# One block of weights and biases for each expert, and three buffers for the dense items: a graph network and a mixture of experts in one launch

## The chip, the cores and the metric

The kernel runs on one core of a Trainium2 chip. The metric is the device time of one execution in microseconds (us); lower is better. Each comparison is against runs of the kernel before on the same chip.

## The reference

Sixteen graphs of 512 nodes with 128 features go through two residual layers, x = x + gnn(layernorm(x)) and x = x + ffn(layernorm(x)), in float32. The second layer is the one that the change is about:

```
xn = (x - mu) * rsqrt(var + EPS) * gamma + beta
top_vals, top_idx = top_k(xn @ Wr + br, 2)          # 2 of 8 experts for each of 8192 tokens
w_full = one_hot-weighted softmax(top_vals)
for e in range(8):
    h = gelu(xn @ W1[e] + b1[e])                    # 128 -> 256
    y_e = h @ W2[e] + b2[e]                         # 256 -> 128
    y = y + y_e * w_full[..., e, None]
```

The first layer is, for each graph, two convolutions over the nodes (17 taps in the second), a message step over a 512x512 matrix exp(-dist) * adj, and a GRU cell with gates from both.

## The kernel before, in words

One program is written by hand for the five engines, with explicit semaphores. TensorE (PE) does the products and transposes, ScalarE (ACT) the gelus and the copies out of PSUM, VectorE (DVE) the splits of float32 values into two parts, the layer norms and the router, GpSimd (POOL) the indirect DMAs, SyncE (SP) issues every other DMA, each engine in the order in which its program is written. An engine's program is in order: what stands behind a wait waits too.

**Graph loop.** `iteration(g)` runs 16 times. Besides graph g's network it finishes graph g-1 (`tail`), routes its tokens, and writes their normalized rows to the lists of their experts in HBM (`routed`). From graph 4 on (`FIRST`) it also works on four **tiles** (`SLOTS`) of 256 routed rows, each with one expert's weights. A tile needs three loads, which SP issues a graph ahead in `tile_loads`: its rows (`xt`, 144 KB), `w1_t` (256 KB: W1 in a high and a low part) and `w2_t` (136 KB: W2, b1, b2 and a one-hot row). Which expert and which rows are read from a small table with two `value_load`s. There are `RING` = 8 buffers of each. On PE a tile is `turn` (transposes of `xt`), `hidden` (six products with W1, lines 573 to 575; waits for `w1_in`), `second` (W2, line 598; behind the gelu) and `back` (transposes, line 606). DVE weighs the result and POOL adds it to the output rows.

**Last stage.** Behind the graph loop stand 50 items, numbered 48 to 97: the last 18 tiles (tiles 48 to 65), and 32 **dense items**, in which each expert's weights are put to all 512 tokens of the last two graphs (q = 0 and 1) in halves of 256, with no routing. The order is worked out in `last_items`. PE runs at step i: `turn` of item i+2 (tiles only), `hidden` or `dense_hidden` of item i+1, `second` of item i, `back` of item i-1. A dense item's weights come in ten loads (`DENSE_LOADS`), each for the two or four items of one expert. They go into two buffers (`wd1`, `wd2`, by k % 2):

```
load k                       0   1   2   3   4   5   6   7   8   9
first item that reads it    53  56  59  66  73  79  86  90  94  96
last item that reads it     54  58  64  71  78  84  89  93  95  97
```

`dense_loads(k)` waits until the last item of load k-2 is through (`pe_y`, `yT_done`), then issues two DMAs. Loads 0 and 1 are issued behind the graph loop, before the stores of padding rows; the others stand in one order with the tiles' loads (`loads_in_order`, sorted by the item that each waits for): tiles 48 to 60, **load 2**, tile 61, tile 62, load 3, tiles 63 and 64, load 4, tile 65, loads 5 to 9. Tiles 48 to 55 wait for POOL's adds (`added`), later ones for items. `dense_hidden` waits for `wd1_in`, `xd_split` and the gelu of an earlier item; ACT's gelu of a dense item waits for `wd2_in`.

**The blocks in HBM** are written once: at graph 0 and 1, ACT and DVE fill `w1_s` and `w2_s` in SBUF (W1 scaled by gamma and split, W2, the biases), and SP stores them with two DMAs (lines 461 and 462) into `w1_all` and `w2_all`; the first tile's loads wait for that (`w12_stored`).

At step AT_NORM = 6 and AT_ROUTE = 9 of the last stage (items 54 and 57) the last graph's rows are normalized and its router's logits are computed (line 777); DVE's `choose` and `place`, at steps 10 and 11, turn them into weights.

Of the kernel before, what the change touches and what calls it, by code (L numbers as in the profile page):

```python
# [15 lines left out]
P = 128  # L16
# [80 lines left out]
W1COLS = 4 * P  # L97
X_B1 = 2 * P
X_B2 = X_B1 + HALVES
X_OH = X_B2 + 1  # L100
XCOLS = 272
# [43 lines left out]
def gnn_moe(nc, x, adj_t, weights, vectors, consts, pads, routed, w1_all, w2_all, out):  # L145
# [4 lines left out]
    with ExitStack() as ctx:  # L150
# [22 lines left out]
        w1_t = [sb(f"w1_t{i}", [P, W1COLS], F32R) for i in range(RING)]  # L173
        w2_t = [sb(f"w2_t{i}", [P, XCOLS]) for i in range(RING)]
# [7 lines left out]
        wd1 = [sb(f"wd1_{i}", [P, W1COLS], F32R) for i in range(2)]  # L182
        wd2 = [sb(f"wd2_{i}", [P, XCOLS]) for i in range(2)]
# [147 lines left out]
        wd1_in = [sem(f"wd1_in{i}") for i in range(2)]  # L331
        wd2_in = [sem(f"wd2_in{i}") for i in range(2)]
        xt_in = [sem(f"xt_in{i}") for i in range(RING)]
        w1_in = [sem(f"w1_in{i}") for i in range(RING)]
        w2_in = [sem(f"w2_in{i}") for i in range(RING)]
# [74 lines left out]
        def _(sp):  # L410
# [14 lines left out]
            sp.dma_start(w2_s[:, :, 0:2 * P],  # L425
# [16 lines left out]
            def dense_loads(k):  # L442
                if k >= 2:
                    sp.wait_ge(pe_y, last_of_load(k - 2) + 1)
                    sp.wait_ge(yT_done, last_of_load(k - 2) + 1)
                e = DENSE_LOADS[k][0]
                sp.dma_start(wd1[k % 2][:].bitcast(F32), w1_all[e, :, :]).then_inc(wd1_in[k % 2], 16)
                sp.dma_start(wd2[k % 2][:], w2_all[e, :, :]).then_inc(wd2_in[k % 2], 16)

            def iteration(g, tail, more, moe):  # L450
                d = g - 1

                def next_loads(j):
                    n, slot, loads = tile_of(g + 1, j)
                    if n >= RING:
                        sp.wait_ge(added, 16 * TT * (n - RING + 1))
                    tile_loads(slot, *chosen[j])

                if g == 1:
                    sp.wait_ge(w12_ready, 2)  # L460
                    sp.dma_start(w1_all.rearrange("e p h -> p e h"), w1_s[:].bitcast(F32)).then_inc(w12_stored, 16)
                    sp.dma_start(w2_all.rearrange("e p h -> p e h"), w2_s[:]).then_inc(w12_stored, 16)
                if tail:
                    sp.wait_ge(x1_ready, d + 1)
                    if d < ROUTED:
                        sp.dma_start(out_v[d], x1[:]).then_inc(out_set, 16)
                if more:
                    sp.wait_ge(a_prod, NT * g + NT)
                    sp.dma_start(adj[:], adj_v[g + 1]).then_inc(adj_loaded, 16)
                if g < GRAPHS - 2:  # L470
                    sp.wait_ge(xl_ready, g + 2)
                    sp.dma_start(x_ln[:], x_v[g + 2]).then_inc(x_ln_loaded, 16)
                if FIRST - 1 <= g < GRAPHS - 1:

                    sp.wait_ge(tab_step, TAB_STEPS * (g - 2))
                sp.dma_start(x_res[:], x_v[g]).then_inc(x_res_loaded, 16)
                if g == FIRST - 1:
# [15 lines left out]
            for k in range(2):  # L493
                dense_loads(k)
# [31 lines left out]
        def _(pe):  # L526
# [97 lines left out]
            def iteration(g, tail, more, moe):  # L624
# [10 lines left out]
                def tile_b(j):  # L635
                    if moe:
                        second(tile_of(g, j)[0], w2_t[tile_of(g, j)[1]])
# [115 lines left out]
            for i in range(-2, len(items) + 1):  # L753
# [9 lines left out]
                if 0 <= i < len(items):  # L763
                    item = items[i]
                    second(item[0], w2_t[item[2]] if is_tile(item) else wd2[item[4] % 2])
# [16 lines left out]
        def _(act):  # L782
# [15 lines left out]
            def gelu(m, w2):  # L798
# [3 lines left out]
                for h in range(HALVES):  # L802
                    last = nc.scalar.activation(ge[m % 2][:, h, :], HID[bank_set(m)][:, h * TILE:(h + 1) * TILE], ACT.Gelu,  # L803
                                                bias=w2[:, X_B1 + h:X_B1 + h + 1])
                last.then_inc(gelu_done, 1)

            def results(m, w2):
# [3 lines left out]
                nc.scalar.activation(yT[m % 2][:], YO[bank_set(m)][:, 0:TILE], ACT.Identity,  # L811
                                     bias=w2[:, X_B2:X_B2 + 1]).then_inc(yT_done, 1)
# [27 lines left out]
            def iteration(g, tail, more, moe):  # L840
# [6 lines left out]
                def tile_gelu(j):  # L847
                    if moe:
                        n, slot, loads = tile_of(g, j)
                        act.wait_ge(w2_in[slot], loads)  # L850
                        gelu(n, w2_t[slot])

                def tile_results(j):
                    n = tile_of(g, 0)[0] + j
                    if moe and n >= 0:
                        results(n, w2_t[n % RING])
# [31 lines left out]
                if is_graph(g, 0):  # L888
                    act.wait_ge(w1_loaded, 16)
                    nc.scalar.activation(w1_s[:, :, 0:2 * P], w1_raw[:].rearrange("p (e h) -> p e h", e=EXPERTS),  # L890
# [47 lines left out]
            results(STREAMED - 1, w2_t[(STREAMED - 1) % RING])  # L938
            for i in range(-2, len(items)):
# [117 lines left out]
        def _(dve):  # L1057
# [300 lines left out]
            def iteration(g, tail, more, moe):  # L1358
# [5 lines left out]
                if is_graph(g, 1):  # L1364
                    dve.wait_ge(w1_hi, 1)
                    nc.vector.scalar_tensor_tensor(
                        out=w1_s[:, :, 2 * P:4 * P], in0=w1_raw[:].rearrange("p (e h) -> p e h", e=EXPERTS),
                        scalar=vec[:, V_GAMMA:V_GAMMA + 1], in1=w1_s[:, :, 0:2 * P].bitcast(F32), op0=ALU.mult,
# [3 lines left out]
                    nc.vector.tensor_tensor(w2_s[:, :, X_B1:X_B1 + HALVES],  # L1372
# [3 lines left out]
                    nc.vector.tensor_copy(w2_s[:, :, X_B2], vec[:, V_EB2:V_EB2 + EXPERTS])  # L1376
                    nc.vector.tensor_copy(w2_s[:, :, X_OH:X_OH + EXPERTS],
                                          cst[:, C_OH:C_OH + 64].rearrange("p (e f) -> p e f", f=EXPERTS))
                    nc.vector.memset(w2_s[:, :, X_OH + EXPERTS:], 0.0).then_inc(w12_ready, 1)
# [243 lines left out]
```

## Time and profile before

| | |
|---|---|
| device time, 3 runs | median 666.71 us (663.08 to 667.06) |
| the profiled execution | 669.05 us, of which the span of the trace is 667.3 us |
| granted TensorE clock, mean over the span | 0.987 |
| busy: PE, its weight loads, DVE, ACT, POOL | 93%, 79%, 75%, 63%, 52% of the span |
| HBM read, written | 75.85 MB, 30.51 MB |
| DMA issued by SP | 83.28 MB in 82736 packets |

The profiled execution is 2.3 us above the median of the runs. Times inside the trace are counted from the start of the span. A granted clock of 1.00 is 2.4 GHz, 0.5 is 1.2 GHz. "Idle before" is the time that an engine stood still before an instruction, and behind the arrow is what the trace takes for its releaser; "issue" is said where the trace shows none. SP's DMA issues are listed with the time that SP took to issue them, not with their landing.

### The profile page before, as it was taken

What the parts mean: (1) busy time and instruction counts of PE and PEld (TensorE: products, weight loads), DVE (VectorE), ACT (ScalarE), POOL (GpSimd) and SP (SyncE); (2) the same over time, 40 slices, a digit from 0 to 9 for tenths busy, and PEclk for the clock granted to TensorE, in tenths of its full rate; (3) what the DMA queues carried; (4) which work ended last, traced back from release to release, by engine and by line L of the source; (5) the groups of instructions that cost most, each with busy time, mean ns of one, the idle gap of its engine ahead of it and who ended that gap; (6) DMA issues with size and microseconds to landing.
All of it is one profiled execution on the core that took longest, in us unless ns stands there. A gap on an engine that the chain in (4) does not pass through costs nothing.

```text
span 667.3 us, 13068 instructions
## 1 busy us (share of the span) xinstructions
PE 623.3 (93%) x3784; PEld 530.2 (79%) x3784; DVE 498.2 (75%) x2050; ACT 418.4 (63%) x824; POOL 344.6 (52%) x273
## 2 busy tenths in 40 slices
PE   3799898989999999999999999999999988799996
PEld 2679687777979797979797888888888777688874
DVE  6958888888888888888888888888888755333322
ACT  4544546485858485858485858585767546466663
POOL 3200314145847474748474747574757545556750
PEclk9898999999999999999999999999999979899999
DMA  8327231538379747474755666666555578863341
GB/s 305 115 92 245 82 124 52 179 101 232 75 203 340 195 117 189 122 191 120 182 130 152 154 153 159 156 156 158 149 140 153 147 184 200 224 144 53 52 77 57
DMA packets 105399, 101.04 MB, mean 151 GB/s; under 512 B 8896, under 2 KB 83904, under 8 KB 105024
## 3 DMA queue, kind: packets, MB, share of 16 engines
q1 hardware_dynamic: 82736, 83.28, 40.4%
q0 software_dynamic: 22592, 16.92, 16.7%
q8 instruction: 31, 0.51, 0.3%
q14 instruction: 40, 0.33, 0.1%
HBM read 75.85 MB, written 30.51 MB: 159 GB/s over the span
## 4 chain that ended last, share of the span: by engine, by line
PE 63%; DVE 17%; issue 7%; DMA 5%; POOL 4%; ACT 3%; SPq 0%; another core or an unknown queue 0%; DVEq 0%; ACTq 0%; POOLq 0%
PE Y L598 9%; PE G L708 5%; PE C L530 5%; PE C L531 5%; PE C L532 5%; PE G L530 4%; PE G L532 4%; PE G L531 4%; PE G L598 4%; POOL routed L1013 2%; DMA x_ln<-x 2%; DMA out<-y_t,xt 2%; PE H L573 2%; PE Y L606 2%; PE H L574 2%
## 5 line engine op out<-in xcount | busy, mean ns | idle before, releaser
L978 POOL DMA_INDIRECT out<-y_t,xt x96 | 157.5, 1641 | 130.7 <-DMA out<-y_t,xt 85.9
L1013 POOL DMA_INDIRECT routed<-row,at_u x112 | 118.6, 1059 | 119.8 <-DVE at_u L1207 86.9
L530 PE MATMUL C<-cv_h,w_hi 128*128 128x256 f32 (+1 forms) x432 | 131.2, 304 | 2.2 <-DVE cv_l L1068 1.3
L531 PE MATMUL C<-cv_l,w_hi 128*128 128x256 f32 (+1 forms) x432 | 124.5, 288 | 0.0
L532 PE MATMUL C<-cv_h,w_lo 128*128 128x256 f32 (+1 forms) x432 | 124.3, 288 | 0.0
L530 PEld LDWEIGHTS C<-cv_h,w_hi 128*128 128x128 f32 x432 | 82.7, 191 | 4.8 <-issue 2.2
L531 PEld LDWEIGHTS C<-cv_l,w_hi 128*128 128x128 f32 x432 | 82.7, 191 | 1.3
L532 PEld LDWEIGHTS C<-cv_h,w_lo 128*128 128x128 f32 x432 | 82.7, 191 | 0.7
L598 PE MATMUL Y<-ge,w_t 128*128 128x256 f32 x228 | 62.0, 395 | 6.0 <-DVE y_t L1307 3.5
L708 PE MATMUL G<-ex,msg_t 128*128 128x512 f32 x128 | 58.9, 603 | 0.3 <-ACT gh L901 0.3
L598 PEld LDWEIGHTS Y<-ge,w_t 128*128 128x128 f32 x228 | 39.4, 192 | 24.0 <-issue 20.5
L803 ACT ACTIVATE ge<-H,w_t 128x256 f32<-128x256 f32 x114 | 47.8, 473 | 5.9 <-PE H L575 5.4
L708 PEld LDWEIGHTS G<-ex,msg_t 128*128 128x128 f32 x128 | 23.1, 190 | 23.5 <-issue 23.0
L910 ACT CAST cv_h<-G 128x512 fp32r<-128x512 f32 x16 | 9.4, 586 | 51.4 <-PE G L708 51.4
L530 PE MATMUL G<-xlT_h,w_hi 128*128 128x512 f32 x96 | 39.9, 415 | 1.5 <-DVE xlT_l L1138 1.5
L1413 DVE TENSOR_TENSOR ex<-ex,adj 128x512 f32<-128x512 f32 x64 | 39.7, 677 | 0.0
L532 PE MATMUL G<-xlT_h,w_lo 128*128 128x512 f32 x96 | 38.3, 399 | 0.0
L531 PE MATMUL G<-xlT_l,w_hi 128*128 128x512 f32 x96 | 38.2, 398 | 0.0
L573 PE MATMUL H<-xT_h,w_t 128*128 128x256 f32 x114 | 36.3, 319 | 0.6 <-DVE xT_l L1286 0.6
L811 ACT ACTIVATE yT<-Y,w_t 128x256 f32<-128x256 f32 x57 | 26.9, 472 | 12.1 <-PE Y L598 8.5
L575 PE MATMUL H<-xT_h,w_t 128*128 128x256 f32 x114 | 32.5, 285 | 0.0
L574 PE MATMUL H<-xT_l,w_t 128*128 128x256 f32 x114 | 32.4, 284 | 0.0
(264 smaller groups left out, 1692.8 us busy)
## 6 DMA issues: line engine op xcount, KB each, us to landing
w_t<-w_all SPq DMA_DIRECT2D x66, 256.0 KB
adj<-adj_t SPq DMA_DIRECT2D x16, 1024.0 KB
xt<-routed SPq DMA_DIRECT2D x66, 144.0 KB
w_t<-w_all SPq DMA_DIRECT2D x66, 136.0 KB
x_ln<-x SPq DMA_DIRECT2D x16, 256.0 KB, 6.3
x_res<-x SPq DMA_DIRECT2D x16, 256.0 KB
out<-x SPq DMA_DIRECT2D x15, 256.0 KB
wd<-w_all SPq DMA_DIRECT2D x10, 256.0 KB
```

Source lines behind the costliest of these rows:

```text
L530: pe.matmul(psum, hi(w), rhs_h, start=start, stop=False)
L531: pe.matmul(psum, hi(w), rhs_l, start=False, stop=False)
L532: return pe.matmul(psum, lo(w), rhs_h, start=False, stop=stop)
L573: pe.matmul(half, w[:, h * P:(h + 1) * P], x_h, start=True, stop=False)
L574: pe.matmul(half, w[:, h * P:(h + 1) * P], x_l, start=False, stop=False)
L575: last = pe.matmul(half, w[:, (2 + h) * P:(3 + h) * P], x_h, start=False, stop=True)
L598: last = pe.matmul(YO[bank_set(m)][:, 0:TILE], w2[:, h * P:(h + 1) * P], ge[m % 2][:, h, :], start=(h == 0), stop=(h == HALVES - 1))
L708: last = pe.matmul(G0[:], msg_t[:, j, :], ex[:, j, :], start=(j == 0), stop=(j == NT - 1))
L803: last = nc.scalar.activation(ge[m % 2][:, h, :], HID[bank_set(m)][:, h * TILE:(h + 1) * TILE], ACT.Gelu, bias=w2[:, X_B1 + h:X_B1 + h + 1])
L978: nc.gpsimd.indirect_dma_start(out=out, out_offset=bass.IndirectOffsetOnAxis(ap=xt[j][:, t, R_ID:R_ID + 1].bitcast(U32), axis=0), in_=y_t[ ...
L1013: nc.gpsimd.indirect_dma_start(out=routed, out_offset=bass.IndirectOffsetOnAxis(ap=at_u[:, n:n + 1], axis=0), in_=row[:, n // TOP, :], in_ ...
L1413: nc.vector.tensor_tensor(ex[:, j, :], ex[:, j, :], adj[:, j, :], ALU.mult).then_inc(a_prod, 1)
```

## The change

The four column ranges of an expert's block are put side by side in one row of 784 floats (3136 bytes): W1 high and low, W2, b1, b2 and the one-hot row. `w1_s` and `w2_s` become `w_s`, `w1_all` and `w2_all` become `w_all`, `w1_t` and `w2_t` become `w_t`. The size is what both had together (2048 + 1088 bytes a row). One DMA stores the blocks, and one loads a tile's or a dense item's block; there is one semaphore for it, and PE, ACT and DVE all wait for that. The dense items' blocks have three buffers instead of two: load k waits for the last item of load k-3, loads 0 to 2 are issued behind the graph loop, and in the order of the rest load 3 stands where load 2 stood, 4 where 3 stood, and so on. All products, activations and vector operations keep their shapes and order.

```diff
@@ -94,11 +94,13 @@
-W1COLS = 4 * P
-X_B1 = 2 * P
+X_W2 = 4 * P
+X_B1 = X_W2 + 2 * P
 X_B2 = X_B1 + HALVES
 X_OH = X_B2 + 1
-XCOLS = 272
+XCOLS = X_B1 + 16
...
+DENSE_BUFFERS = 3
@@ -164,14 +166,12 @@
             w1_raw = once("w1_raw", [P, 16 * P])
-            w1_s = once("w1_s", [P, EXPERTS, W1COLS], F32R)
-            w2_s = once("w2_s", [P, EXPERTS, XCOLS])
+            w_s = once("w_s", [P, EXPERTS, XCOLS], F32R)
             beta_b = once("beta_b", [P, P])
...
         xt = [sb(f"xt{i}", [P, TT, ROW]) for i in range(RING)]
-        w1_t = [sb(f"w1_t{i}", [P, W1COLS], F32R) for i in range(RING)]
-        w2_t = [sb(f"w2_t{i}", [P, XCOLS]) for i in range(RING)]
+        w_t = [sb(f"w_t{i}", [P, XCOLS], F32R) for i in range(RING)]
         yT = [sb(f"yT{i}", [P, TILE]) for i in range(2)]
@@ -179,8 +179,7 @@
         own_w = [sb(f"own_w{i}", [P, TT]) for i in range(4)]
-        wd1 = [sb(f"wd1_{i}", [P, W1COLS], F32R) for i in range(2)]
-        wd2 = [sb(f"wd2_{i}", [P, XCOLS]) for i in range(2)]
+        wd = [sb(f"wd{i}", [P, XCOLS], F32R) for i in range(DENSE_BUFFERS)]
         xd_h = [sb(f"xd_h{i}", [P, NODES], F32R) for i in range(DENSE)]
@@ -396,7 +393,7 @@
-            at = [(last_of_load(k - 2), 1, k) for k in range(2, len(DENSE_LOADS))]
+            at = [(last_of_load(k - DENSE_BUFFERS), 1, k) for k in range(DENSE_BUFFERS, len(DENSE_LOADS))]
             at += [(number.get(n - RING, STREAMED), 0, n) for n in range(STREAMED, STREAMED + LAST)]
@@ -430,9 +427,8 @@
                     xt_in[j], 16)
-                sp.dma_start(w1_t[j][:].bitcast(F32), w1_all[bass.ds(e, 1), :, :].rearrange("e p h -> p (e h)")).then_inc(
-                    w1_in[j], 16)
-                sp.dma_start(w2_t[j][:], w2_all[bass.ds(e, 1), :, :].rearrange("e p h -> p (e h)")).then_inc(w2_in[j], 16)
+                sp.dma_start(w_t[j][:].bitcast(F32), w_all[bass.ds(e, 1), :, :].rearrange("e p h -> p (e h)")).then_inc(
+                    w_in[j], 16)
@@ -440,12 +436,12 @@
             def dense_loads(k):
-                if k >= 2:
-                    sp.wait_ge(pe_y, last_of_load(k - 2) + 1)
-                    sp.wait_ge(yT_done, last_of_load(k - 2) + 1)
+                if k >= DENSE_BUFFERS:
+                    sp.wait_ge(pe_y, last_of_load(k - DENSE_BUFFERS) + 1)
+                    sp.wait_ge(yT_done, last_of_load(k - DENSE_BUFFERS) + 1)
                 e = DENSE_LOADS[k][0]
-                sp.dma_start(wd1[k % 2][:].bitcast(F32), w1_all[e, :, :]).then_inc(wd1_in[k % 2], 16)
-                sp.dma_start(wd2[k % 2][:], w2_all[e, :, :]).then_inc(wd2_in[k % 2], 16)
+                sp.dma_start(wd[k % DENSE_BUFFERS][:].bitcast(F32), w_all[e, :, :]).then_inc(
+                    wd_in[k % DENSE_BUFFERS], 16)
@@ -458,8 +454,7 @@
                     sp.wait_ge(w12_ready, 2)
-                    sp.dma_start(w1_all.rearrange("e p h -> p e h"), w1_s[:].bitcast(F32)).then_inc(w12_stored, 16)
-                    sp.dma_start(w2_all.rearrange("e p h -> p e h"), w2_s[:]).then_inc(w12_stored, 16)
+                    sp.dma_start(w_all.rearrange("e p h -> p e h"), w_s[:].bitcast(F32)).then_inc(w12_stored, 16)
                 if tail:
@@ -475,7 +470,7 @@
                 if g == FIRST - 1:
-                    sp.wait_ge(w12_stored, 32)
+                    sp.wait_ge(w12_stored, 16)
                     sp.wait_ge(pads_stored, 16)
@@ -490,7 +485,7 @@
-            for k in range(2):
+            for k in range(DENSE_BUFFERS):
                 dense_loads(k)
@@ -578,25 +573,25 @@
                 pe.wait_ge(xT_split, n + 1)
-                pe.wait_ge(w1_in[j], loads)
+                pe.wait_ge(w_in[j], loads)
                 if m > 0:
                     pe.wait_ge(gelu_done, m if m <= STREAMED else m - 1)
-                hidden_products(HID[bank_set(m)], w1_t[j], xT_h[n % 2][:], xT_l[n % 2][:])
+                hidden_products(HID[bank_set(m)], w_t[j], xT_h[n % 2][:], xT_l[n % 2][:])
...
                 pe.wait_ge(xd_split, q + 1)
-                pe.wait_ge(wd1_in[k % 2], 16 * (k // 2 + 1))
+                pe.wait_ge(wd_in[k % DENSE_BUFFERS], 16 * (k // DENSE_BUFFERS + 1))
                 pe.wait_ge(gelu_done, m - 1)
                 cols = slice(u * TILE, (u + 1) * TILE)
-                hidden_products(HID[bank_set(m)], wd1[k % 2], xd_h[q][:, cols], xd_l[q][:, cols])
...
-            def second(m, w2):
+                hidden_products(HID[bank_set(m)], wd[k % DENSE_BUFFERS], xd_h[q][:, cols], xd_l[q][:, cols])
...
+            def second(m, w):
                 pe.wait_ge(gelu_done, m + 1)
...
                 for h in range(HALVES):
-                    last = pe.matmul(YO[bank_set(m)][:, 0:TILE], w2[:, h * P:(h + 1) * P], ge[m % 2][:, h, :],
-                                     start=(h == 0), stop=(h == HALVES - 1))
+                    last = pe.matmul(YO[bank_set(m)][:, 0:TILE], w[:, X_W2 + h * P:X_W2 + (h + 1) * P].bitcast(F32),
+                                     ge[m % 2][:, h, :], start=(h == 0), stop=(h == HALVES - 1))
                 last.then_inc(pe_y, 1)
@@ -943,14 +938,14 @@
                     if is_tile(item):
-                        act.wait_ge(w2_in[item[2]], item[3])
-                        gelu(item[0], w2_t[item[2]])
+                        act.wait_ge(w_in[item[2]], item[3])
+                        gelu(item[0], w_t[item[2]])
                     else:
-                        act.wait_ge(wd2_in[item[4] % 2], 16 * (item[4] // 2 + 1))
-                        gelu(item[0], wd2[item[4] % 2])
+                        act.wait_ge(wd_in[item[4] % DENSE_BUFFERS], 16 * (item[4] // DENSE_BUFFERS + 1))
+                        gelu(item[0], wd[item[4] % DENSE_BUFFERS])
                 if i >= 0:
                     item = items[i]
-                    results(item[0], w2_t[item[2]] if is_tile(item) else wd2[item[4] % 2])
+                    results(item[0], w_t[item[2]] if is_tile(item) else wd[item[4] % DENSE_BUFFERS])
                 if i == AT_SUM + 2:
@@ -1287,10 +1282,10 @@
             def own_weight(n, j, loads):
-                dve.wait_ge(w2_in[j], loads)
+                dve.wait_ge(w_in[j], loads)
                 dve.wait_ge(xt_in[j], loads)
                 nc.vector.tensor_tensor(pick_w[n % 4][:], xt[j][:, :, R_W:R_W + EXPERTS],
-                                        over(w2_t[j][:, X_OH:X_OH + EXPERTS], 1, [P, TT, EXPERTS]),
+                                        over(w_t[j][:, X_OH:X_OH + EXPERTS].bitcast(F32), 1, [P, TT, EXPERTS]),
                                         ALU.mult).then_inc(own_step, 1)
...
```

## Rows read from the trace of the kernel before

**Rows 1.** Busy time by stretch: from:to, length, PE, PEld, DVE, ACT, POOL, clock, DMA share, GB/s.
```profile
461.30:494.90 33.60, 33.45 (x211) 28.70 (x211) 28.81 (x125) 23.26 (x47) 21.45 (x16) 1.00 0.59 148
538.80:549.00 10.20, 7.86 (x33) 6.51 (x33) 5.23 (x19) 4.33 (x11) 4.67 (x3) 0.67 0.79 208
...
571.50:580.40 8.90, 4.47 (x20) 3.73 (x19) 1.27 (x6) 1.68 (x4) 6.54 (x6) 0.81 0.96 239
580.40:654.30 73.90, 71.64 (x442) 61.85 (x441) 28.28 (x119) 49.23 (x117) 43.23 (x39) 1.00 0.46 82
654.30:667.30 13.00, 7.15 (x38) 5.49 (x38) 3.14 (x10) 4.33 (x10) 0.00 (x0) 1.00 0.25 72
```

**Rows 2.** Waits of PE in the last stage: total us, times, longest.
```profile
PE G L573 <- issue: 4.4, 1, 4.4
...
PE H L573 <- issue: 0.9, 1, 0.9
```

**Rows 3.** SP's issues in order of time: start us, us to issue.
```profile
517.13 0.46 SPq L448 DMA_DIRECT2D wd<-w_all  x1
...
536.09 0.41 SPq L431 DMA_DIRECT2D xt<-routed  x1
...
538.88 0.38 SPq L431 DMA_DIRECT2D xt<-routed  x1
539.46 0.33 SPq L433 DMA_DIRECT2D w_t<-w_all  x1
539.97 0.33 SPq L435 DMA_DIRECT2D w_t<-w_all  x1
...
572.28 0.38 SPq L447 DMA_DIRECT2D wd<-w_all  x1
...
653.82 0.33 SPq L447 DMA_DIRECT2D wd<-w_all  x1
```

**Rows 4.** PE in order of time, last stage: start us, us, [idle before].
```profile
545.18 0.56 PE L573 MATMUL G<-xT_h,w_t 128*128 128x256 f32 x1
...
571.33 0.42 PE L541 MATMUL H<-cst,xt 128*128 128x128 f32 x2
576.18 0.50 PE L573 MATMUL G<-xd_h,wd 128*128 128x256 f32 x1 [4.43 <-issue]
...
582.82 1.10 PE L598 MATMUL Y<-ge,w_t 128*128 128x256 f32 x4
...
652.13 1.10 PE L598 MATMUL G<-ge,wd 128*128 128x256 f32 x4 [0.16 <-DVE x_d L1320]
...
654.32 1.10 PE L598 MATMUL Y<-ge,wd 128*128 128x256 f32 x4 [0.15 <-DVE x L1320]
...
656.49 0.36 PE L573 MATMUL H<-xd_h,wd 128*128 128x256 f32 x1 [0.86 <-issue]
...
657.28 1.03 PE L598 MATMUL G<-ge,wd 128*128 128x256 f32 x4
...
659.51 1.10 PE L598 MATMUL Y<-ge,wd 128*128 128x256 f32 x4 [0.27 <-DVE x L1320]
```

**Rows 5.** DVE in order of time behind the long wait.
```profile
579.87 0.42 DVE L1307 TENSOR_TENSOR adj<-G,own_w 128x256 f32<-128x256 f32 x1 [6.90 <-PE G L606]
...
582.06 0.61 DVE L1320 SCALAR_TENSOR_TENSOR x_d<-Y,w_d,x_d 128x128 f32<-128x128 f32 x2
```

**Rows 6.** The last instruction of POOL in order of time.
```profile
643.37 1.56 POOL L999 DMA_INDIRECT out<-x_ln,ids  x1 [0.30 <-issue]
```

**Rows 7.** SP and PE in order of time: a graph's first tile, issue and use.
```profile
328.37 0.35 SPq L433 DMA_DIRECT2D w_t<-w_all  x1
...
338.89 0.47 PE L573 MATMUL H<-xT_h,w_t 128*128 128x256 f32 x1
```

**Rows 8.** The `x_ln` tile: issue to landing of its loads, 256 KB each.
```profile
DMA to landing us min/median/max: 2.8/6.3/7.5
```

**Rows 9.** DMA issues by line: the second of the two stores, us to landing.
```profile
w_all<-w_s SPq DMA_DIRECT2D x1, 1088.0 KB, 11.6
```

More of the change, by code:

```diff
@@ L142, in pad_rows, with gnn_moe @@
     return r
-def gnn_moe(nc, x, adj_t, weights, vectors, consts, pads, routed, w1_all, w2_all, out):
+def gnn_moe(nc, x, adj_t, weights, vectors, consts, pads, routed, w_all, out):
     x_v = x.rearrange("g (t p) d -> g p t d", p=P)
@@ L330, in gnn_moe @@
         tab_step, xd_hi, xd_split = map(sem, ("tab_step", "xd_hi", "xd_split"))
-        wd1_in = [sem(f"wd1_in{i}") for i in range(2)]
-        wd2_in = [sem(f"wd2_in{i}") for i in range(2)]
+        wd_in = [sem(f"wd_in{i}") for i in range(DENSE_BUFFERS)]
         xt_in = [sem(f"xt_in{i}") for i in range(RING)]
-        w1_in = [sem(f"w1_in{i}") for i in range(RING)]
-        w2_in = [sem(f"w2_in{i}") for i in range(RING)]
+        w_in = [sem(f"w_in{i}") for i in range(RING)]
         pe_xtT, xT_hi, xT_split, pe_h, gelu_done, pe_y, yT_done, pe_yT, own_step, own_done, y_done, added = map(
@@ L424, in _ @@
             sp.dma_start(w1_raw[:], weights[:, W1 * P:(W1 + 16) * P]).then_inc(w1_loaded, 16)
-            sp.dma_start(w2_s[:, :, 0:2 * P],
+            sp.dma_start(w_s[:, :, X_W2:X_W2 + 2 * P].bitcast(F32),
                          weights[:, W2 * P:(W2 + 16) * P].rearrange("p (e h) -> p e h", e=EXPERTS)).then_inc(w2_loaded, 16)
@@ L636, in tile_b @@
                     if moe:
-                        second(tile_of(g, j)[0], w2_t[tile_of(g, j)[1]])
+                        second(tile_of(g, j)[0], w_t[tile_of(g, j)[1]])
                 if is_graph(g, 1):
@@ L764, in _ @@
                     item = items[i]
-                    second(item[0], w2_t[item[2]] if is_tile(item) else wd2[item[4] % 2])
+                    second(item[0], w_t[item[2]] if is_tile(item) else wd[item[4] % DENSE_BUFFERS])
                 if 0 <= i - 1:
@@ L796, in turned, with gelu @@
                 nc.scalar.copy(xT_h[n % 2][:], XT[s][:, 0:TILE]).then_inc(xT_hi, 1)
-            def gelu(m, w2):
+            def gelu(m, w):
                 act.wait_ge(pe_h, m + 1)
@@ L803, in gelu, with results @@
                     last = nc.scalar.activation(ge[m % 2][:, h, :], HID[bank_set(m)][:, h * TILE:(h + 1) * TILE], ACT.Gelu,
-                                                bias=w2[:, X_B1 + h:X_B1 + h + 1])
+                                                bias=w[:, X_B1 + h:X_B1 + h + 1].bitcast(F32))
                 last.then_inc(gelu_done, 1)
-            def results(m, w2):
+            def results(m, w):
                 act.wait_ge(pe_y, m + 1)
@@ L811, in results @@
                 nc.scalar.activation(yT[m % 2][:], YO[bank_set(m)][:, 0:TILE], ACT.Identity,
-                                     bias=w2[:, X_B2:X_B2 + 1]).then_inc(yT_done, 1)
+                                     bias=w[:, X_B2:X_B2 + 1].bitcast(F32)).then_inc(yT_done, 1)
             def normalized_rows(d):
@@ L849, in tile_gelu @@
                         n, slot, loads = tile_of(g, j)
-                        act.wait_ge(w2_in[slot], loads)
-                        gelu(n, w2_t[slot])
+                        act.wait_ge(w_in[slot], loads)
+                        gelu(n, w_t[slot])
                 def tile_results(j):
@@ L855, in tile_results @@
                     if moe and n >= 0:
-                        results(n, w2_t[n % RING])
+                        results(n, w_t[n % RING])
                 act.wait_ge(pe_s, g + 1)
@@ L889, in iteration @@
                     act.wait_ge(w1_loaded, 16)
-                    nc.scalar.activation(w1_s[:, :, 0:2 * P], w1_raw[:].rearrange("p (e h) -> p e h", e=EXPERTS),
+                    nc.scalar.activation(w_s[:, :, 0:2 * P], w1_raw[:].rearrange("p (e h) -> p e h", e=EXPERTS),
                                          ACT.Copy, scale=vec[:, V_GAMMA:V_GAMMA + 1]).then_inc(w1_hi, 1)
@@ L937, in _ @@
             d = GRAPHS - 1
-            results(STREAMED - 1, w2_t[(STREAMED - 1) % RING])
+            results(STREAMED - 1, w_t[(STREAMED - 1) % RING])
             for i in range(-2, len(items)):
@@ L1366, in iteration @@
                     nc.vector.scalar_tensor_tensor(
-                        out=w1_s[:, :, 2 * P:4 * P], in0=w1_raw[:].rearrange("p (e h) -> p e h", e=EXPERTS),
-                        scalar=vec[:, V_GAMMA:V_GAMMA + 1], in1=w1_s[:, :, 0:2 * P].bitcast(F32), op0=ALU.mult,
+                        out=w_s[:, :, 2 * P:4 * P], in0=w1_raw[:].rearrange("p (e h) -> p e h", e=EXPERTS),
+                        scalar=vec[:, V_GAMMA:V_GAMMA + 1], in1=w_s[:, :, 0:2 * P].bitcast(F32), op0=ALU.mult,
                         op1=ALU.subtract).then_inc(w12_ready, 1)
@@ L1371, in iteration @@
                     dve.wait_ge(pe_b1, 1)
-                    nc.vector.tensor_tensor(w2_s[:, :, X_B1:X_B1 + HALVES],
+                    nc.vector.tensor_tensor(w_s[:, :, X_B1:X_B1 + HALVES].bitcast(F32),
                                             H0[:, 0:16].rearrange("p (e h) -> p e h", h=HALVES),
@@ L1375, in iteration @@
                                             ALU.add).then_inc(b1_set, 1)
-                    nc.vector.tensor_copy(w2_s[:, :, X_B2], vec[:, V_EB2:V_EB2 + EXPERTS])
-                    nc.vector.tensor_copy(w2_s[:, :, X_OH:X_OH + EXPERTS],
+                    nc.vector.tensor_copy(w_s[:, :, X_B2].bitcast(F32), vec[:, V_EB2:V_EB2 + EXPERTS])
+                    nc.vector.tensor_copy(w_s[:, :, X_OH:X_OH + EXPERTS].bitcast(F32),
                                           cst[:, C_OH:C_OH + 64].rearrange("p (e f) -> p e f", f=EXPERTS))
-                    nc.vector.memset(w2_s[:, :, X_OH + EXPERTS:], 0.0).then_inc(w12_ready, 1)
+                    nc.vector.memset(w_s[:, :, X_OH + EXPERTS:].bitcast(F32), 0.0).then_inc(w12_ready, 1)
                 def tile_split(j):
@@ L1616 @@
     routed = nc.dram_tensor("routed", (DUMMY + LAST * TILE, ROW), F32, kind="Internal").ap()
-    w1_all = nc.dram_tensor("w1_all", (EXPERTS, P, W1COLS), F32, kind="Internal").ap()
-    w2_all = nc.dram_tensor("w2_all", (EXPERTS, P, XCOLS), F32, kind="Internal").ap()
+    w_all = nc.dram_tensor("w_all", (EXPERTS, P, XCOLS), F32, kind="Internal").ap()
     out = nc.dram_tensor("out", (TOKENS + LAST * TILE, P), F32, kind="ExternalOutput").ap()
-    gnn_moe(nc, *args, routed, w1_all, w2_all, out)
+    gnn_moe(nc, *args, routed, w_all, out)
     result = run_bass_kernel_spmd(nc, [arrays], core_ids=[0])
```

## The prediction

> **What bounds the kernel now.** I read the busy time by stretch first, because the share over the whole span hides the stages [rows 1]. In the graph loop a graph takes 33.6 us and PE is busy in 33.45 of them at the full clock: only less PE work could shorten it, and the change takes none away. The last stage is different. PE is busy in 4.47 of 8.9 us between 571.5 and 580.4, in 7.86 of 10.2 between 538.8 and 549, and in 7.15 of the last 13. In the two low stretches the granted clock was 0.81 and 0.67, so TensorE went partly at 1.2 GHz. Next come the waits of PE in that stage [rows 2]: the longest is one of 4.4 us ahead of line 573, and line 573 also has one of 0.9 us. Both have "issue" as releaser, which says only that the trace names none. PE's rows in order of time [rows 4] show both in front of a `dense_hidden` (it reads `xd_h` and `wd`), at 576.18 and at 656.49, and SP's rows [rows 3] show a `wd` load issued shortly before each: at 572.28 (load 2) and at 653.82 (load 9). The other things that `dense_hidden` waits for, the split rows and an earlier gelu, were there long before. So I take both for waits on loads, issue to first product 3.9 and 2.67 us. Why they are issued late is in the code. Load 2 stands in SP's queue behind thirteen tiles' loads, and SP needs 2.79 us for a tile (536.09 to 538.88 [rows 3]). Load 9 has to wait for item 93 to leave its buffer and is read by item 96.
>
> **The third buffer, load 2.** Load 2 goes out beside loads 0 and 1, whose last issue is at 517.13 [rows 3], some 59 us before it is read. The long wait goes. The transposes ahead of it start at 571.33 and take some 0.15 us of PE's time when it doesn't stop, so `dense_hidden` of item 59 can start at about 571.5. What follows would run as in the undisturbed part. From the start of six products to the `second` behind them is 0.79 us (656.49 to 657.28). An item costs 2.10 us (582.82 is `second` of item 60, 654.32 that of item 94: 71.5 us over 34 items) [rows 4]. `second` of item 60 is then due at 571.5 + 0.79 + 2 x 2.10 = 576.5. It was at 582.82, so **6.3 us** are won. Of these 4.7 are the wait itself. The other 1.6 are the work behind it that went at 1.2 GHz: the first product behind the wait takes 0.50 us, the same one at 656.49 takes 0.36 [rows 4]. From 580.4 to 654.3, with PE at work, the clock was 1.00 [rows 1]; without the standstill I see nothing to lower it.
>
> What is late next there? DVE's router work for the last graph. DVE begins to weigh item 57 at 579.87 and its weighing of item 58 starts at 582.06, ends at 582.67, and `second` of item 60 starts right behind, at 582.82 [rows 5, 4]. This is a chain of 2.95 us from `back` of item 57, and it moves forward with that. `back` of item 57 would end at about 571.5 + 0.8 (six products) + 1.0 (`second`) + 0.4 (two transposes, 0.42 at 571.33) = 573.7, so DVE allows item 60 at 576.7. That takes 0.2 away: **6.1 us**.
>
> **The third buffer, load 9.** It now waits for item 89, seven items before it is read, or 15 us, against the 2.67 that it needs. The last items stand 2.19 us apart (652.13 and 654.32, `second` of items 93 and 94). At that pace item 96 would come at 654.32 + 4.38 = 658.70; it came at 659.51 [rows 4], so **0.8 us** are won. Loads 3 to 8 had five to nine items of lead and get ten to fifteen; PE shows no third wait of this kind [rows 2], so they bring nothing.
>
> **One load for two.** SP saves one issue for each tile, 539.97 - 539.46 = 0.51 us [rows 3], so over thirteen tiles its queue gets 6.6 us shorter until POOL's adds hold it up. With load 2 out of the queue no item waits for SP. Cover: PE's own work. In the graph loop SP saves 2 us a graph beside a full PE: nothing. Against that, `hidden` now waits for the whole block, where it waited for W1 alone. The block is issued where W1 was, and it can't land later than W2's load did, if the bytes move at the same pace; so `hidden` waits for at most 0.5 us more than now. The tightest tile is 49: issue of W1 at 539.46, products at 545.18, 5.7 us [rows 3, 4] against 3.9 for the slowest dense load. In the loop a first tile has 10.5 us (328.37 to 338.89 [rows 7]). Bounds: nothing, and a gain of up to 1 us if the stretch from 538.8 to 549 is held by these loads in part. I take nothing.
>
> **The stores, the writes in `w_s`, the added issue.** One store for two of the same bytes; the second of the two took 11.6 us to land [rows 9] around 65 us, and its first reader is issued at 127. Between nothing and 0.3 us in the graphs where SP issues it; I take nothing. The vector writes go to rows with another pitch, with the same elements: nothing. The third dense load adds about 0.5 us to SP at 518, in a pause before the padding stores. PE's weights and ACT's biases come from the same kind of buffer.
>
> **The end.** POOL's last add starts at 643.37 [rows 6] and would be over at 645; the new end of PE's work is near 657, so POOL isn't next. The final store behind the last item stays.
>
> **Sum.** 6.1 + 0.8 = 6.9 us. The profiled execution took 669.05, so it would take 662.15; the median of the runs is 2.3 lower, and I subtract the same from it: 666.71 - 6.9 = **659.8 us**, 1.03% less.
>
> **A rule beside it.** The Trainium skill, "DMA: Bandwidth & Descriptors", section "Anatomy of one DMA", gives a DMA some 2.0 us plus its bytes at 436 GB/s; by that load 2 (256 KB) would have been ready 2.6 us after its issue, at 574.9. The trace agrees for load 9 (2.67) and not for load 2 (3.9, in a stretch with a DMA share of 0.96 [rows 1]). An estimate from that page makes the wait 3.4 us, and the sum 5.6 us and not 6.9.
>
> **Rivals.**
> (B) *The wait is shorter in a usual execution.* Load 2 met busy DMA engines. If it lands as load 9 did, in 2.67 us, PE waits 1.2 us less; the clock may then also stay up for part of the work behind it. The gain is 4.2 to 5.7 us: 661 to 662.5. For it: the runs are faster than the profiled execution by 2.3 us, and something in them must be shorter. Against it: the same queue order and the same traffic exist in each of them. The Trainium skill, "TensorE: Matmul & The Clock Gate", section "Part 1: The HAM clock gate", says that the point at which the clock changes varies from run to run with the same kernel; no run here shows that yet. By that the 1.5 us for the clock could be anything between nothing and all of it.
> (C) *Another wait takes the place.* DVE's `choose` and ACT's gap step now come while PE is at full pace; if their chain of 2.95 us grows by one item, or the clock falls all the same, 2 to 3 us are given back: about 662.5.
> (D) *The releaser isn't the load.* The trace names none. Then only load 9's 0.8 us are left: 665.9. Against it stand two pairs of issue and start.
> (E) *Shorter queue, more gain.* If the stretch from 538.8 to 549 is held by tile loads, up to 1 us, and the clock's share behind it, up to 2: 657.
> (F) *Slower.* The joint block lands late where only W1 was waited for. Place: the first tile of eleven graphs (all with tiles but the first) and tiles 49 to 52. Price: every microsecond by which a block needs more than 10.5 us costs 11 us in the loop [rows 7]; above 5.7 us each of tiles 49 to 52 waits too, and the clock falls. Loads of 256 KB that stand behind others took up to 7.5 us to land [rows 8]; if time went with bytes, 392 KB would take 11.5: 1 us x 11 and some 5 us in the last stage, less 6.9, so 9 us slower, about 676. It decides from a latency of about 11 us. Against it: dense loads took 2.67 and 3.9 us with the second half issued right behind.
>
> **Chances.** My sum 0.52, with a range of its own from 658 to 661.5; B 0.19, C 0.09, D 0.07, E 0.08, F 0.05. A measurement of this kernel can tell about 1% from no change, and 1% is 6.67 us: the bound of "faster", 660.04, goes through the middle of my own case. A bit over half of it, E, and a little of B make 0.43 for faster; the rest of it, B, C and D make 0.52 for within 1%; F is slower, 0.05. The range must hold my sum, B, C and most of E, with the 2 us by which medians of this kernel move: 656.5 to 664.5.
>
> **What would show it.** In the changed kernel's trace PE has no wait over 1 us in front of a product with `wd`; `wd` has ten issues, the third near 518; the clock between 571 and 580 is 1.00, that of 538.8 to 549 is still near 0.67; `second` of item 60 comes 5.4 us behind the transposes that start at 571.33 now (11.5 now); in the last 13 us PE's wait of 0.86 is gone; a graph still takes 33.6 us. Wrong would be: a wait of the same length at the same product (D), a wait of PE on `w_t` at tiles 49 to 52 or at a graph's first tile (F), or a new DVE or ACT wait at items 59 to 62 (C).

## The result, and the profile after

The changed kernel took 668.95 us (median of 11 runs, 666.59 to 672.55), the kernel before 665.76 us (11 runs, 663.08 to 668.61). The ratio is 1.0056, 95% interval 1.0039 to 1.0074: **3.2 us slower**, where I had forecast 6.9 us faster. Now and then an execution falls into a slower state; every ratio here is of the others. The profiled execution of the changed kernel took 667.68 us, with a span of 665.9.

The busy time by stretch of the changed kernel (columns as in [rows 1]; line numbers in its trace are 5 lower than in the kernel before) shows both halves of the story. The last graph's message products begin at 536.2 here and at 528.9 before, so the fourth and fifth stretch are those of [rows 1] moved by 7.3 us, to hold the same work:

```profile
187.90:223.30 35.40, 33.63 (x211) 28.70 (x211) 29.17 (x125) 23.22 (x46) 19.21 (x14) 1.00 0.88 264
223.30:267.90 44.60, 34.99 (x212) 29.84 (x211) 28.66 (x125) 23.27 (x46) 25.59 (x18) 0.89 0.63 167
...
301.40:335.00 33.60, 33.45 (x211) 28.71 (x211) 28.69 (x125) 23.26 (x46) 21.83 (x16) 1.00 0.60 156
...
546.10:556.30 10.20, 7.61 (x50) 6.35 (x50) 6.42 (x24) 5.71 (x14) 3.52 (x3) 1.00 0.92 250
...
578.80:587.70 8.90, 8.62 (x56) 7.39 (x55) 5.38 (x34) 5.83 (x15) 4.09 (x5) 1.00 0.92 264
...
654.30:665.90 11.60, 5.71 (x32) 4.23 (x30) 3.14 (x10) 3.31 (x8) 0.00 (x0) 0.91 0.15 30
```

The fifth is what I had forecast for the last stage: no standstill, full clock. The fourth has the full clock too, which I had not forecast. But two graphs in the loop, 187.9 to 223.3 and 223.3 to 267.9, took 35.4 and 44.6 us, and every other one of this kind 33.6 (as 301.4 to 335). That is 1.8 + 11.0 = 12.8 us more. From PE's first product on line 708 (703 here) of the last graph to PE's end it is 134.9 us before and 125.4 after, 9.4 less. 12.8 - 9.4 = 3.4 us, near the 3.2 us between the medians. The spans of the two profiled executions don't show this sum: 667.3 before and 665.9 after. The kernel before lost another 5.5 us ahead of the last stage in its profiled execution (the start and a few graphs, one of 35.1 us among them), and the changed kernel's end behind PE's last product was 0.7 us longer. That execution was 3.3 us above its kernel's median, the changed kernel's 1.3 below.

The waits of PE over the whole span, as in [rows 2], name the new one. Neither wait of [rows 2] is left:

```profile
PE G L536 <- ACT row L816: 11.3, 3, 9.5
PE M L531 <- DVE xl L1127: 5.5, 1, 5.5
```

ScalarE's `row` step (`normalized_rows`) waits for `rows_out`: it writes the tile that POOL's scatter of the last graph's rows still reads. Its own rows in order of time say so:

```profile
216.61 1.65 ACT L816 ACTIVATE row<-x,nb,rs 128x128 f32<-128x128 f32 x4 [2.53 <-DMA routed<-row,at_u]
259.87 1.65 ACT L816 ACTIVATE row<-x,nb,rs 128x128 f32<-128x128 f32 x4 [10.35 <-DMA routed<-row,at_u]
```

The chain of waits (start us, us, what), read backwards from there, goes through POOL for 70 us and begins with one DMA:

```profile
191.59 1.56 POOL out L973
193.45 12.09 DMA out<-y_t,xt
206.30 1.92 POOL out L973
208.53 4.20 DMA out<-y_t,xt
...
215.50 3.00 POOL out L973
218.80 6.16 DMA out<-y_t,xt
225.71 1.55 POOL out L973
227.57 6.42 DMA out<-y_t,xt
234.75 1.55 POOL out L973
...
238.48 0.99 POOL routed L1008
...
253.32 6.47 DMA routed<-row,at_u
```

An add of a tile to the output (`add`, two indirect DMAs) must land before POOL begins the next. The one issued at 193.45 took 12.09 us, where the others here took 4.20 to 6.42. POOL began the next tile's add only at 206.30. By the next graph it was a whole tile behind: its row scatter began at 238.48, 50.6 us behind PE's first message product of graph 5, where it is 41.4 us in the same kernel without the stores (experiment 2). The scatter's last DMA was issued at 253.32, just behind the load of the next `adj`, and took 6.47 us to land. SP's issues in order of time show what went out with the slow add, and with the last scatter:

```profile
193.21 0.38 SPq L430 DMA_DIRECT2D w_t<-w_all  x1
193.64 0.57 SPq L482 DMA_DIRECT2D routed<-pads  x1
194.26 0.64 SPq L483 DMA_DIRECT2D out<-pads  x1
...
252.21 0.38 SPq L464 DMA_DIRECT2D adj<-adj_t  x1
```

The first is weights, the second **the padding store** of graph 5 (line 487 before): 2016 KB from `pads` into the dummy rows of `routed`, both contiguous in HBM. The third is 1792 KB of padding into the output's spare rows (line 488 before). In the kernel before, SP and POOL in order of time had them apart:

```profile
199.48 0.65 SPq L487 DMA_DIRECT2D routed<-pads  x1
200.18 0.58 SPq L488 DMA_DIRECT2D out<-pads  x1
```
```profile
197.17 1.56 POOL L978 DMA_INDIRECT out<-y_t,xt  x1 [0.30 <-issue]
199.03 0.99 POOL L1013 DMA_INDIRECT routed<-row,at_u  x1 [0.30 <-issue]
...
204.39 1.73 POOL L978 DMA_INDIRECT out<-y_t,xt  x1 [0.31 <-issue]
```

Before, the store was issued 2.3 us behind the add's second DMA (197.17), and POOL could go on at 204.39. Now it goes out 0.2 us behind it, since SP needs 4.3 us from the first of the four tiles' loads to the store, where it needed 7.0.

### The profile page after: what moved, and what is told of

It reads as the page before. It is cut to its first block, busy times and chain, and to the rows that moved or that the text cites. A ratio compares the mean times of both kernels' runs of the same rounds, so it can differ in the third digit from the quotient of the medians.

```text
span 665.9 us, 12858 instructions
## 1 busy us (share of the span) xinstructions
PE 619.6 (93%) x3784; PEld 527.4 (79%) x3784; DVE 496.7 (75%) x2050; ACT 417.9 (63%) x824; POOL 345.7 (52%) x273
## 4 chain that ended last, share of the span: by engine, by line
PE 69%; DVE 12%; DMA 7%; issue 4%; POOL 4%; ACT 4%; SPq 0%; DVEq 0%; ACTq 0%; POOLq 0%
PE Y L593 10%; PE C L525 6%; PE C L527 6%; PE C L526 6%; PE G L703 5%; DMA out<-y_t,xt 4%; PE G L525 4%; PE G L527 4%; PE G L593 4%; PE G L526 4%; POOL out L973 2%; PE Y L601 2%; PE H L568 2%; PE H L570 2%; PE H L569 2%
## 5 line engine op out<-in xcount | busy, mean ns | idle before, releaser
L1133 DVE TENSOR_TENSOR xlT_l<-M,xlT_h 128x512 fp32r<-128x512 f32 x16 | 11.1, 692 | 36.1 <-ACT xlT_h L826 36.1
L816 ACT ACTIVATE row<-x,nb,rs 128x128 f32<-128x128 f32 x60 | 24.8, 494 | 18.7 <-DMA routed<-row,at_u 12.9
L568 PE MATMUL H<-xT_h,w_t 128*128 128x256 f32 x114 | 35.8, 314 | 0.8 <-DVE xT_l L1281 0.8
```

The lines of the kernel that those rows point to most:

```text
L568: pe.matmul(half, w[:, h * P:(h + 1) * P], x_h, start=True, stop=False)
L816: last = nc.scalar.activation(row[:, t, 0:P], x1_of(d)[:, t, :], ACT.Identity, scale=rs[:, t:t + 1], bias=nb[:, t:t + 1])
```

## The experiments

**Theory P**: the joint load moves the padding stores up against POOL's add; POOL falls behind; ScalarE and PE wait for the scatter. The third buffer has no part in it and gains what I had worked out. **Rivals**: T, it comes with the third buffer; D, the 3136-byte rows of the joint load slow POOL's DMAs by themselves.

**1. The parts of the change one by one.** First the joint block with two buffers:

```diff
-DENSE_BUFFERS = 3
+DENSE_BUFFERS = 2
```

> The changed kernel with two buffers for the dense items instead of three. Theory P (padding stores): with the joint loads SP issues the two large padding stores of graph 5 earlier against POOL's adds, POOL falls one tile behind, and its row scatter lands late for graph 7: ScalarE's row step waits some 10 us, PE 9.5. That has nothing to do with the third buffer, so it stays, and the two waits of the last stage (4.4 and 0.9 us, with the slow clock behind) come back: 669 + 7 = about 676. Theory T (third buffer): the new wait comes with the third buffer or the shifted addresses behind it; then this one is like the kernel before, 665 to 667.

677.16 us, ratio 1.0162 (1.0132 to 1.0192). Its waits of PE have all three:

```profile
PE G L536 <- ACT row L816: 10.8, 3, 10.1
...
PE G L568 <- issue: 4.4, 1, 4.4
```

The third, of 1.8 us (0.9 before), is on the other half of line 568. So the joint block alone costs 10.8 us, and T falls.

Then the kernel before with three buffers for `wd1` and `wd2`, and the two loads as they were (beside these lines, each `k % 2` becomes `k % DENSE_BUFFERS`):

```diff
-                if k >= 2:
-                    sp.wait_ge(pe_y, last_of_load(k - 2) + 1)
+                if k >= DENSE_BUFFERS:
+                    sp.wait_ge(pe_y, last_of_load(k - DENSE_BUFFERS) + 1)
```

> The kernel before, two loads for each block as they were, with three buffers for the dense items. Theory P: no wait of ScalarE on the row scatter over 1 us, the two waits of the last stage gone: 6.9 us less than before, 659. Theory T: the wait of about 9.5 us in graph 7 appears here: 668 to 669. If the last stage's gain is less than I worked out, between 660 and 664.

659.11 us, ratio 0.9905 (0.9878 to 0.9933), by the ratio 6.3 us less than before. No wait of ScalarE on the scatter.

**2. The padding stores moved away.** Both go out in graph 2, where POOL has no adds:

```diff
-                if g == FIRST + 1:
+                if g == 2:
                     sp.dma_start(routed[DUMMY + TAKEN:, :], pads[TAKEN:, :]).then_inc(pads_stored, 16)
                     sp.dma_start(out[TOKENS + TAKEN:, :], pads[TAKEN:, 0:P]).then_inc(pads_stored, 16)
```

and the wait ahead of the first tile's loads is for 48 instead of 16. In the changed kernel:

> The changed kernel with the two large padding stores (2016 and 1792 KB) moved from graph 5 to graph 2, where POOL has no adds. Theory P: no late row scatter at graph 7, 9.5 us less than the changed kernel in its profiled run, 658 to 660. Theory D (descriptors): the 3136-byte rows of the joint loads slow POOL's DMAs by themselves; then ScalarE still waits for the row scatter somewhere and the time stays at 666 to 669.

657.21 us, ratio 0.9872 (0.9847 to 0.9898). All graphs with tiles and a successor take 33.6 us. In the kernel before:

> The kernel before with the same two stores moved to graph 2. Theory P: before had only a 1 us wait of ScalarE on the scatter at graph 6, so this gains at most 1 to 2 us: 664 to 666. Theory D says the same; it is the reference for e3. If it gains as much as e3 against its own base, the padding stores cost the kernel before something too.

665.37 us, ratio 0.9992 (0.9968 to 1.0016). The same edit is worth 1.8% in the changed kernel and nothing that can be seen in the one before.

**3. The moment alone.** In the changed kernel SP waits for an event of graph 5 ahead of the stores, so that they go out later:

```diff
                 if g == FIRST + 1:
+                    sp.wait_ge(z_tanh, g + 1)
```

> The changed kernel, in which SP waits in graph 5 for the graph's second gate before the two padding stores, so that they are issued some 3 us later against POOL's adds, about as in the kernel before. Theory P (it is the moment of their issue against POOL's second add of a tile): no late row scatter, 657 to 660. Theory D (3136-byte rows): the wait of 10 us stays, 666 to 669.

Ratio 0.9908 (0.9843 to 0.9973). It rests on two executions only, of 663.53 and 667.24 us, on a chip on which the kernel before takes 672.81 us. ScalarE still waits for the scatter twice, 2.8 us in all, but PE's waits on ScalarE's `row` are down to 0.8 us, with the joint block in place: D falls. And the reverse, two loads and three buffers (the second kernel above), with the stores ahead of the fourth tile's loads:

```diff
+                        if g == FIRST + 1 and j == SLOTS - 1:
+                            sp.dma_start(routed[DUMMY + TAKEN:, :], pads[TAKEN:, :]).then_inc(pads_stored, 16)
+                            sp.dma_start(out[TOKENS + TAKEN:, :], pads[TAKEN:, 0:P]).then_inc(pads_stored, 16)
...
-                if g == FIRST + 1:
-
-                    sp.dma_start(routed[DUMMY + TAKEN:, :], pads[TAKEN:, :]).then_inc(pads_stored, 16)
-                    sp.dma_start(out[TOKENS + TAKEN:, :], pads[TAKEN:, 0:P]).then_inc(pads_stored, 16)
```

> Two loads for each block and three buffers (e2, 659), with the two padding stores issued ahead of the fourth tile's loads in graph 5, some 1.6 us earlier than in e2, right behind POOL's second DMA of an add. Theory P: the add's landing is held up by 5 us and more, the row scatter is late and PE waits 10 us with no joint block in the kernel: 668. Theory D: nothing changes, 659.

677.88 us, ratio 1.0089 (1.0034 to 1.0143), on the same chip. The long wait is there without any joint block, and a graph earlier than in the changed kernel (the stretch from graph 5 takes 44.4 us and the next 33.6; why it comes sooner stays open):

```profile
PE G L541 <- ACT row L821: 7.8, 1, 7.8
```

**4. Which store, and what of it.** In the changed kernel only the first store is moved to graph 2 (the wait is for 32):

> The changed kernel with only the first of the two stores (2016 KB into the expert lists, 64512-byte packets) moved to graph 2; the second (1792 KB, 512-byte packets) stays in graph 5. If the large packets hold up POOL's add, the wait is gone: 657 to 660. If it is the mere number of bytes ahead of it in the DMA engines, part or all of it stays: 662 to 669.

Ratio 0.9899 (0.9854 to 0.9944), 664.48 us, again on the slower chip: the wait is gone. Then only the second store:

> The changed kernel with only the second store (1792 KB to the output's spare rows, 512-byte packets) moved to graph 2; the first (2016 KB, 64512-byte packets) stays in graph 5. If the large packets hold up POOL's add by themselves, ScalarE still waits for the row scatter, though a shorter one is possible since half the bytes are gone: ratio to before 1.000 to 1.006. If both stores are needed for it, ratio 0.988 as e3 and e8.

668.38 us, ratio 1.0069 (1.0038 to 1.0099):

```profile
PE G L537 <- ACT row L817: 10.9, 3, 9.7
```

The first store does it by itself. Last, both stores stay in graph 5 and the first keeps its bytes and its moment, but in pieces of a row:

```diff
-                    sp.dma_start(routed[DUMMY + TAKEN:, :], pads[TAKEN:, :]).then_inc(pads_stored, 16)
+                    sp.dma_start(routed[DUMMY + TAKEN:, :].rearrange("(n p) c -> p n c", p=P),
+                                 pads[TAKEN:, :].rearrange("(n p) c -> p n c", p=P)).then_inc(pads_stored, 16)
```

> The changed kernel with both stores where they were, but the first in rows of 576 bytes instead of 64512-byte packets: the same bytes and the same moment. If the size of the packets is what keeps POOL's add back, its landing takes the usual 5 to 6 us and the ratio to before is 0.987 to 0.991. If it is the bytes queued ahead, the wait of some 10 us stays, 1.000 to 1.006. Many small packets to HBM could also make it worse.

657.17 us, ratio 0.9891 (0.9861 to 0.9922). POOL and SP in order of time:

```profile
194.39 1.56 POOL L974 DMA_INDIRECT out<-y_t,xt  x1 [0.30 <-issue]
...
201.76 1.61 POOL L974 DMA_INDIRECT out<-y_t,xt  x1 [0.64 <-issue]
```
```profile
194.25 0.94 SPq L482 DMA_DIRECT2D routed<-pads  x1
195.24 8.16 SPq L484 DMA_DIRECT2D out<-pads  x1
```

Same moment, same bytes, and POOL's next add starts after 7.4 us. This edit changes two things, though: the packets are small, and SP hands them over more slowly (its next issue took 8.16 us), so they don't come in one burst. The first kernel of this experiment helps there. Its remaining store, 1792 KB in packets of 512 bytes, took SP 0.57 us to issue, 0.4 us ahead of the add's second DMA, and POOL's next add came after 7.3 us. So neither the moment nor the bytes do it alone, and the size of the packets is what the harmful cases have in common.

The kernels side by side, from rows like these. "Apart" is from the start of the add's second DMA to the issue of the first large store, "next add" is how long after that second DMA POOL began the next tile's add. The 7.0 to 7.4 us are POOL's own pace (that DMA and four of the scatter), with the add's landing within them:

| kernel | add's second DMA | store issued | apart | next add | ratio |
|---|---|---|---|---|---|
| before | 197.17 | 199.48 | +2.3 | 7.2 | 1 |
| three buffers only | 193.65 | 195.88 | +2.2 | 7.2 | 0.9905 |
| changed, stores later | 199.69 | 201.15 | +1.5 | 7.4 | 0.9908 |
| three buffers, stores ahead | 200.06 | 200.78 | +0.7 | 12.4 | 1.0089 |
| changed | 193.45 | 193.64 | +0.2 | 12.9 | 1.0056 |
| changed, two buffers | 194.45 | 194.28 | -0.2 | 11.6 | 1.0162 |
| changed, second store moved | 194.07 | 193.89 | -0.2 | 11.9 | 1.0069 |
| changed, store in 576-byte pieces | 194.39 | 194.25 | -0.1 | 7.4 | 0.9891 |
| changed, first store moved | 197.68 | 197.31 (the second) | -0.4 | 7.3 | 0.9899 |
| changed, both stores in graph 2 | 194.08 | none | | 7.0 | 0.9872 |

**5. What is the joint block worth without the collision?** The two kernels with both stores in graph 2, three buffers, one with two loads for each block and one with the joint one. First the one with two loads:

> Two loads for each block as before, three buffers, both large padding stores at graph 2: e3 without the joint block. If the joint block is worth nothing once the padding stores are out of the way, this equals e3, 657 to 658. If the shorter queue of SP is worth something, e3 is faster than this by 1 us or more.

Ratio 0.9913 (0.9873 to 0.9953), 665.53 us beside 672.81. Then both again, on one chip:

> e3 once more (joint block, three buffers, both stores at graph 2), now on one chip with the same without the joint block (e12). If the joint block is worth nothing where the stores are out of the way, both have the same ratio to before, 0.987 to 0.991, with less than 1.5 us between them.

656.07 us, ratio 0.9876 (0.9851 to 0.9901).

> e5 once more (two loads for each block, three buffers, both stores at graph 2), beside e11. Within 1.5 us of e11 if the joint block is worth nothing; slower than e11 by 1 to 3 us if SP's shorter queue gives something to the graph loop or the last stage.

658.14 us, ratio 0.9916 (0.9892 to 0.9941). Joint is 2.1 us faster, and 0.4% was also the distance of the first pair. The two intervals still overlap, so the sign is likely and not settled. One could look for the place in a wait of PE for a tile's rows in the last stage, which two of the kernels with two loads have, the second of experiment 1 and this one:

```profile
PE G L542 <- DMA xt<-routed: 1.6, 1, 1.6
```
```profile
PE G L542 <- DMA xt<-routed: 1.2, 1, 1.2
```

In the joint kernel of this pair it is absent, but the second kernel of experiment 4, with the joint block, has it too:

```profile
PE H L537 <- DMA xt<-routed: 1.2, 1, 1.2
```

and the first kernel of this experiment, with two loads, hasn't. So this wait is not shown to be the place. From the last graph's message product to PE's end the traces have 126.5 us on average over the seven kernels with the joint block and three buffers, and 127.5 over the four with two loads; that is a difference of 1 us with a spread of 2 in either group.

The fastest version is the changed kernel with both padding stores in graph 2: 1.2 to 1.3% under the kernel before, on two chips.

## Why the prediction was wrong, point by point

- **What bounds the last stage; loads 2 and 9.** Right. PE in order of time, behind the transposes that stood ahead of the long wait (571.33 before, [rows 4]):

```profile
576.21 0.41 PE L536 MATMUL H<-cst,xt 128*128 128x128 f32 x2
576.38 0.36 PE L568 MATMUL G<-xd_h,wd 128*128 128x256 f32 x1
...
581.40 1.10 PE L593 MATMUL Y<-ge,w_t 128*128 128x256 f32 x4
```

  No idle time in front of the product, and `second` of item 60 comes 5.2 us behind the transposes; 5.4 was forecast, 11.5 it had been. The product takes 0.36 us and not 0.50, so the clock stayed up as I said. With two buffers (1.0162) against three (1.0056) the joint kernels differ by 1.05%, 7.0 us; without the joint block it is 6.3 us. The sum said 6.9.
- **The releaser** (rival D of the prediction). "Issue" was the load, as argued.
- **One load for two: nothing, covered by PE.** This is the step that failed. I wrote "in the graph loop SP saves 2 us a graph beside a full PE: nothing". A shorter queue doesn't only save SP's time, it also moves everything that stands behind it, and in graph 5 that is the two padding stores. The prediction names only those behind the graph loop. The ones of graph 5 cost nothing that can be seen where they were (experiment 2: 0.9992), and the kernel is 10.8 us slower with the joint block, that is 2.1 to 2.5 us earlier against POOL's add (table). In the changed kernel they cost 1.8%, some 12 us.
- **The stores and the vector writes.** Nothing, and nothing was seen.
- **The rule beside the sum.** The section of the Trainium skill that the prediction names gives it for DMAs that GpSimd issues. Loads 2 and 9 were issued by SP, so the one that agrees (2.67 us) and the one that doesn't (3.9 us) say little of it.
- **POOL isn't next.** I looked at POOL's end only. In the loop it stands close to the edge: from 183 us on, the scatter's last DMA landed at most 3.2 us before ScalarE's `row` began, in every graph of the kernel before. It also had a wait there: `row` at 217.77 waited 0.98 us for the scatter, in the very graph with the stores.

```profile
217.77 1.65 ACT L821 ACTIVATE row<-x,nb,rs 128x128 f32<-128x128 f32 x4 [0.98 <-DMA routed<-row,at_u]
```

  One add that lands some 6 us late costs little in its own graph (1.8 us), and 11 in the next. Each later add waits for the one before it, and the last scatter took 6.47 us to land, beside 2.3 to 5.0 in the graphs behind that one; that the load of the next `adj` made it so slow is argued from their order, not shown.
- **Rival F** had the sign and the wrong mechanism: no product ever waited for a joint block, and its trigger, a latency of 11 us, never came; the joint loads took 4.7 us (median) to land and the dense ones 3.8, a tile's block at most 6.5 us. The range ended at 664.5, since F's 676 was given 0.05 and no rival had a displaced transfer.
- **Rival E** (a shorter queue helps the tight tiles, up to 3 us) is probably real, with about 2 us, and not settled (experiment 5).
- **The clock.** I expected 538.8 to 549 to stay near 0.67. The same work had 1.00 in the changed kernel (546.1 to 556.3), but the change is not what raised it. With two buffers and the joint block it was 1.00 as well (546.8 to 557.0), and in the first kernel of experiment 5, with three buffers, it fell again:

```profile
544.30:554.50 10.20, 7.91 (x32) 6.62 (x33) 5.22 (x19) 4.36 (x11) 4.77 (x4) 0.67 0.78 204
```

  So this fall belongs to the single execution. Of the 9.4 us that the profiled executions gained from the last graph's message product to PE's end, a part is of the same sort. That stage took 134.9, 135.6 and 136.1 us in the traces of the three kernels with two buffers, and 125.4 to 128.4 in those of the eleven with three. The third buffer is therefore worth some 7 to 10 us there in single traces, beside 6.3 and 7.0 by the ratios. In graph 7 of the changed kernel, in turn, the clock was 0.89 over the graph, at 1.2 GHz from 254.1 to 264.3, around the end of the long wait (261.6).

## What to carry to other kernels

When an edit shortens a queue, list what stands behind the shortened part, not only what is in it: the transfer that moves may be the one that was harmless only by its place. Large fills that nobody needs soon belong in a stage where no other engine waits on landings in turn, and not as contiguous copies beside small DMAs with a chain behind them. And of an engine with much idle time, ask for the margin of each wait on it: POOL was busy for 52% of the span, and one add that landed some 6 us late was enough to make the step behind its next graph's scatter wait 10 us.

## What the runs showed of the hardware

- The first store is contiguous on both sides, and the DMA records show it as 32 packets of 64512 bytes that took 2.4 us each (mean 2.45), between 197.39 and 203.82 in the changed kernel; 32 x 2.45 over sixteen DMA engines is 4.9 us of each. Of the 256 packets of 512 bytes of POOL's add in that trace, 132 went before 199.0, 16 from there to 202.5, and 108 behind that. An add issued 0.7 us ahead of the store or less landed 10.9 to 12.1 us after its second DMA began, where the same add took 4.7 to 6.6 in the other kernels; in pieces of 576 bytes the same store did it no harm. The Trainium skill, "DMA: Bandwidth & Descriptors", section "Queues, rings and completion order", says that an engine takes turns between queues only at the end of a packet; the runs agree, for a packet of 64512 bytes as against small ones.
- What is ahead decides: with 1.5 us between them or more, POOL's next add kept its usual 7 us. The edge lies between 0.7 and 1.5.
- The store in small pieces kept SP at its next issue for 8.16 us, where it had been 0.64. It cost nothing in that place, as SP had nothing urgent to issue.
